# Moving small steps between engines in the front body of a state-space layer

## The reference

```python
xr, gate = jnp.split(x @ W_in.T, 2, axis=-1)
xr = xr + t_emb[:, None, :]
xc = jax.nn.silu(conv(xr, W_conv) + b_conv)          # 4 taps in time, each channel by itself
xn = (xc - xc.mean(-1)) / jnp.sqrt(xc.var(-1) + 1e-05) * ln_g + ln_b
Bm, Cm, dt = jnp.split(xn @ W_xproj.T, 3, axis=-1)
dt = jnp.tanh(dt @ W_dt.T + b_dt) * 0.01
Ad = 1.0 + dt * (-jnp.tanh(A_log))
Bd = Bm * jnp.minimum(jnp.linalg.norm(xn, axis=-1, keepdims=True), 1.0)
# scan over time: h = clip(h * ad + bd * xt, -10, 10);  yt = ct . h
y = ys + D * xn
x = x + (y * jax.nn.silu(gate)) @ W_out.T
```

## Time and profile before

| | |
|---|---|
| median of 3 runs | 1788.49 us (1788.26 to 1793.8) |
| span of the profiled execution | 1790.3 us |
| the profiled execution's own time beside its span | the profile gives none; its span is 1.8 us above the median |
| TensorE busy | 1677.0 us, 94% |
| VectorE busy | 1623.9 us, 91% |
| ScalarE busy | 1307.1 us, 73% |
| GpSimd busy | 686.9 us, 38% |
| first root step of the front stage to first scan step, first layer | 568.03 to 743.08 us |

### The profile page before, as it was taken

The page is one execution under the profiler, slowest core; times in us unless marked ns, Lnnn a source line. Parts: engine busy times, 40 slices in busy tenths (PEclk is TensorE's granted clock), DMA queues, the critical chain, the costliest instruction groups (busy, mean ns, idle before and its releaser), DMA issues. The chain is left out here.

```text
span 1790.3 us, 43798 instructions
## 1 busy us (share of the span) xinstructions
PE 1677.0 (94%) x14852; PEld 748.9 (42%) x14852; DVE 1623.9 (91%) x2492; ACT 1307.1 (73%) x2213; POOL 686.9 (38%) x702
## 2 busy tenths in 40 slices
PE   6999999999999999889999999999998899999998
PEld 3555555555554555332222224545553322222244
DVE  5899999999987999989999998679999899999975
ACT  5655556455546999889999993069998899999910
POOL 0223233232332332456666650012335576765500
PEclk9999999999999999899999999999998999999999
DMA  4000001000002344554545666624345445455678
GB/s 162 1 2 0 1 2 31 2 1 0 1 1 83 129 161 163 181 172 133 183 150 188 226 188 205 237 84 173 136 175 185 155 137 184 150 189 196 189 235 276
DMA packets 126456, 226.85 MB, mean 127 GB/s; under 512 B 35620, under 2 KB 61220, under 8 KB 117540
## 3 DMA queue, kind: packets, MB, share of 16 engines
q1 hardware_dynamic: 125912, 223.51, 37.9%
q10 hardware_dynamic: 432, 1.84, 0.3%
HBM read 141.95 MB, written 83.36 MB: 126 GB/s over the span
## 5 line engine op out<-in xcount | busy, mean ns | idle before, releaser
L1063 ACT ACTIVATE R<-q,Ast 128x512 f32<-128x512 f32 x1016 | 632.9, 708 | 34.5 <-DVE q L2085 32.3
L2085 DVE SCALAR_TENSOR_TENSOR q<-R,PS 128x512 f32<-128x512 f32 x1008 | 610.3, 677 | 9.6 <-ACT R L1063 5.9
L628 POOL TENSOR_TENSOR Uw<-Ub,rowmask 96x512 bf16<-96x512 bf16 x256 | 335.6, 1345 | 144.0 <-PE PS L1510 131.7
L1510 PE MATMUL PS<-xq,Uw 97*128 97x512 bf16 x1024 | 327.1, 391 | 46.5 <-DVE q L2085 37.8
L1527 PE MATMUL PS<-q,Wy 128*32 128x512 f32 x2016 | 279.8, 610 | 0.4 <-DVE q L2085 0.4
L1510 PEld LDWEIGHTS PS<-xq,Uw 97*128 97x128 bf16 x1024 | 84.9, 97 | 363.5 <-DVE q L2085 271.4
L1178 PE MATMUL PS<-X,Win 128*128 (+1 forms) x456 | 213.6, 606 | 0.1
L1079 PE MATMUL PS<-xn,Wl 128*128 128x512 f32 x384 | 186.6, 609 | 0.8 <-DVE xn L1649 0.7
L549 POOL TENSOR_TENSOR ex<-ex,rs 128x1024 f32<-128x1024 f32 x32 | 76.8, 2401 | 164.2 <-DVE rs L1672 164.2
L1767 DVE SCALAR_TENSOR_TENSOR acc<-xp,Wc,acc 128x512 f32<-128x512 f32 x192 | 134.5, 749 | 2.6 <-DVE eC L1889 0.2
L542 POOL TENSOR_TENSOR vsc<-vTd,vs_t 128x1024 f32<-128x1024 f32 x16 | 41.6, 2601 | 216.4 <-ACT vTd L773 216.4
(11 more groups left out here) (183 smaller groups left out, 2640.9 us busy)
## 6 DMA issues: line engine op xcount, KB each, us to landing
xq<-xpart_d SPq DMA_DIRECT2D x384, 192.0 KB
sg_d<-sg SPq DMA_DIRECT2D x16, 1024.0 KB, 5.3
xn_d<-z SPq DMA_DIRECT2D x16, 1024.0 KB, 3.9
y_d<-ys SPq DMA_DIRECT2D x64, 256.0 KB, 4.0
xnp<-xn_d SPq DMA_DIRECT2D x16, 1024.0 KB, 8.3
sgp<-sg_d SPq DMA_DIRECT2D x16, 1024.0 KB, 11.1
xpart_d<-xh SPq DMA_DIRECT2D x16, 512.0 KB, 2.9
xpart_d<-xmi SPq DMA_DIRECT2D x16, 512.0 KB, 3.7
```

The lines of the kernel that those rows point to most:

```text
L628: pl.tensor_tensor(Uw[0:XROWS, h, w, :, :, :], Ub[0:XROWS, w, 0:N, ds(s0, CH)].rearrange("p n t -> p t n").unsqueeze(2).broadcast_to([XROW ...
L1063: act.activation((end if end and (h, t) == (1, CH - 1) else R)[:, w, :], q[:, t % 2, w, :], ACT.Relu, scale=Ast[:, h, w, t:t + 1], bias=CL ...
L1510: pe.matmul(PS[:, w, :], Uw[0:KROWS, h, w, t, :, :].rearrange("p b n -> p (b n)"), xq[0:KROWS, hb, w, s8 % XT, :], start=True, stop=True). ...
L2085: v.scalar_tensor_tensor(out=q[:, s8 % 2, w, :], in0=R[:, w, :], scalar=2 * CLIP, in1=PS[:, w, :], op0=ALU.min, op1=ALU.subtract).then_inc ...
```

## The change

It moves steps of the front body from one engine to another and reorders the lists around them.

- `inverse_norm` and VectorE's `over_decay` leave the bodies; GpSimd gets `norm_over_decay`, five steps that give the same `mr`. `carried` goes to GpSimd too.
- In the six looped bodies `split_b` is divided: ScalarE makes the first part (`b_high`), VectorE the next two steps (`b_rest`), GpSimd the last part (`b_low`). In the seventh body it stays whole on VectorE.
- `mean_middle` goes from GpSimd to ScalarE. In the looped bodies two of the four casts of `middle_part` go from ScalarE to GpSimd.
- On VectorE `decay` stands ahead of the last conv product, `rest(it, 3, 3)` ahead of `mean_rows`, and `scaled_b` between the second and third `centred`.
- On ScalarE `high_part(3)` and `mean` stand ahead of `log_norm`, and `tap(it + 1, 3)` ahead of the second gate.
- On TensorE the first gate projection is the one that is split in halves (its first half at the end of the body before), no longer the third; the mean's spread stands ahead of the third input projection.
- SyncE no longer waits for `xmi_r` before it stores the x parts; `xlo_r` stands for it.

```diff
+                def parts_free(it):
                     pl.wait_ge(xq_st, it * 48 + 48)
-                    pl.wait_ge(eC_r, it + 1)
                     alone(pl)
...
+                def middle_part(it, k, cast):
+                    pl.wait_ge(xr1_r, it * TT + k + 1 + TT)
+                    alone(pl)
+                    pl.tensor_copy(xmi[:, k, :], xr1[:, k, :]).then_inc(xmi_r, 1)
+                    pl.wait_ge(xmi_r, cast)
+                    pl.tensor_tensor(xlo[:, k, :], xr1[:, k, :], xmi[:, k, :], ALU.subtract).then_inc(xlo_r, 1)
+
+                def low_part(it, k, cast):
+                    pl.wait_ge(xma_r, cast)
+                    pl.tensor_tensor(xlo[:, k, :], xr1[:, k, :], xmi[:, k, :], ALU.subtract).then_inc(xlo_r, 1)
+
+                def norm_over_decay(it):
+                    pl.wait_ge(n2_r, it + 1)
+                    pl.wait_ge(ng_r, it * 2 + 2)
+                    alone(pl)
+                    pl.tensor_tensor(n3[:, :], n2[:, :], mn[:, :], ALU.mult).then_inc(mn_r, 1)
+                    pl.wait_ge(mn_r, it * 3 + 1)
+                    pl.tensor_tensor(n4[:, :], n3[:, :], mn[:, :], ALU.mult).then_inc(mn_r, 1)
+                    pl.wait_ge(rc_r, it * 4 + 4)
+                    pl.tensor_tensor(n3[:, :], n3[:, :], rc[:, :], ALU.mult).then_inc(mm_r, 1)
+                    pl.wait_ge(mn_r, it * 3 + 2)
+                    alone(pl)
+                    pl.tensor_scalar(n4[:, :], n4[:, :], -0.5, 1.5, ALU.mult, ALU.add).then_inc(mn_r, 1)
+                    pl.wait_ge(mm_r, it + 1)
+                    pl.wait_ge(mn_r, it * 3 + 3)
+                    alone(pl)
+                    pl.tensor_tensor(mr[:, :], n4[:, :], n3[:, :], ALU.mult).then_inc(mr_r, 1)
...
+                def b_low(it):
+                    pl.wait_ge(tv_s, it * 4 + 3)
+                    pl.tensor_tensor(tvp[:, 2, :], tvr[:, :], tvp[:, 1, :], ALU.subtract).then_inc(tv_s, 1)
...
                     over_decay(l * G + g)
-                    mean_middle(l * G + g + 1)
-                    last_parts(l * G + g)
+                    parts_free(l * G + g)
+                    middle_part(l * G + g, 0, g * 2 + (l * (2 * G) + 1))
+                    norm_over_decay(l * G + g)
+                    middle_part(l * G + g, 1, g * 2 + (l * (2 * G) + 2))
+                    carried(l * G + g)
+                    low_part(l * G + g, 2, g * 2 + (l * (2 * G) + 1))
+                    low_part(l * G + g, 3, g * 2 + (l * (2 * G) + 2))
+                    b_low(l * G + g)
...
+                def b_high(it):
+                    act.wait_ge(tv_st, it * (TV_STORES * 16) + TV_STORES * 16)
+                    act.wait_ge(tok_mm, it + 1)
+                    act.activation(tvp[:, 0, :], PS[:, 7, 0:P], ACT.Copy).then_inc(tv_s, 1)
...
                     gate_silu(it + 1, 0)
+                    tap(it + 1, 3)
                     gate_silu(it + 1, 1)
-                    tap(it + 1, 3)
...
                     logarithm_set()
-                    log_norm(it)
                     high_part(it, 3, 3)
                     mean(it + 1)
+                    log_norm(it)
+                    mean_middle(it + 1)
                     minus_c(it)
...
                     square(it + 1, 3)
+                    if ahead:
+                        b_high(it)
...
-                    gate_in(it + 1, g + 1, 0)
                     variance(it, 0, 4)
...
                     x_in_proj(it, g, 3)
+                    gate_half(it + 1, g + 1, 0, 1)
                     gate_in(it + 1, g + 1, 1)
-                    gate_half(it + 1, g + 1, 2, 0)
                     pe.wait_ge(row_r, it * 2 + (2 * AT + 2))
                     spread_out(5, rows3, zb_mm)
-                    gate_half(it + 1, g + 1, 2, 1)
+                    gate_in(it + 1, g + 1, 2)
...
                     if ahead:
                         x_in_proj(it + 1, g + 1, 1)
+                    pe.wait_ge(row_r, it * 2 + (2 * AT + 3))
+                    spread_out(5, rows3, zm_mm)
                     if ahead:
                         x_in_proj(it + 1, g + 1, 2)
-                    pe.wait_ge(row_r, it * 2 + (2 * AT + 3))
-                    spread_out(5, rows3, zm_mm)
+                        gate_half(it + 2, g + 2, 0, 0)
                     fold_b(it)
...
+                    decay(it)
                     conv(it + 1, 2, 3)
-                    decay(it)
...
                     rest(it, 2, 2)
-                    inverse_norm(it)
                     mean_rest(it + 1)
-                    over_decay(it)
-                    scaled_b(it)
-                    carried(it)
+                    rest(it, 3, 3)
                     mean_rows(it + 1)
-                    rest(it, 3, 3)
                     centred(it + 1, 0)
                     centred(it + 1, 1)
+                    scaled_b(it)
                     centred(it + 1, 2)
                     centred(it + 1, 3)
                     if ahead:
                         embed(it + 2, g + 2, 1)
-                    if ahead:
                         embed(it + 2, g + 2, 2)
-                    split_b(it)
+                        b_rest(it)
+                    else:
+                        split_b(it)
```

More of the change, by code:

```diff
@@ L236, in cond_resid_kernel @@
              "xlo_ready", "xparts_stored")]
+        xma_r = sem("xmid_by_scalar")
         dlg_r, dco_g, rg_r, zg_r, ng_r, mm_r = [sem(n) for n in
@@ L577, in _ @@
                 pl.memset(words(pass_tables[0][0]), 0.0).then_inc(tab0_zero, 1)
-                def last_parts(it):
+                def parts_free(it):
                     pl.wait_ge(xq_st, it * 48 + 48)
-                    pl.wait_ge(eC_r, it + 1)
                     alone(pl)
-                    for k in range(TT):
-                        pl.wait_ge(xmi_r, it * TT + k + 1)
-                        pl.tensor_tensor(xlo[:, k, :], xr1[:, k, :], xmi[:, k, :], ALU.subtract).then_inc(xlo_r, 1)
+                def middle_part(it, k, cast):
[4 more added lines that the diff above has]
+                    pl.tensor_tensor(xlo[:, k, :], xr1[:, k, :], xmi[:, k, :], ALU.subtract).then_inc(xlo_r, 1)
@@ new lines, in carried @@
+                def carried(it):
+                    pl.wait_ge(rB_r, it + 1)
+                    pl.tensor_tensor(eC[:, :].rearrange("p (b t) -> p b t", t=S)[:, :, 0:S - 1],
+                                     Cn[:, :].rearrange("p (b t) -> p b t", t=S)[:, :, 0:S - 1],
+                                     rB[:, :].rearrange("p (b t) -> p b t", t=S)[:, :, 1:S], ALU.mult).then_inc(eC_r, 1)
+                def b_low(it):
+                    pl.wait_ge(tv_s, it * 4 + 3)
+                    pl.tensor_tensor(tvp[:, 2, :], tvr[:, :], tvp[:, 1, :], ALU.subtract).then_inc(tv_s, 1)
@@ L605, in std_middle @@
                     pl.wait_ge(rem_r, it * 2 + (2 * AT + 2))
-                    alone(pl)
-                    pl.tensor_copy(middle[:, :], remain[:, :]).then_inc(mid_r, 1)
-                def mean_middle(it):
-                    pl.wait_ge(rem_r, it * 2 + (2 * AT + 1))
                     alone(pl)
@@ L652, in _ @@
                 over_decay(l * G + G - 2)
-                mean_middle(l * G + G - 2 + 1)
+                norm_over_decay(l * G + G - 2)
+                carried(l * G + G - 2)
                 pl.wait_ge(tab_in[0], l * (16 * TABLES) + 16 * TABLES)
@@ L659, in _ @@
                     stage(0, 0, h, True)
-                last_parts(l * G + G - 2)
+                parts_free(l * G + G - 2)
+                for k in range(TT):
+                    low_part(l * G + G - 2, k, l * (2 * G) + 2 * (G - 2) + k + 1)
                 with pl.Fori(1, 4) as c2:
@@ L674, in _ @@
                     for k in (2 * c2, 2 * c2 + 1):
-                        pl.wait_ge(xmi_r, it * TT + k + 1)
+                        pl.wait_ge(xmi_r, l * (2 * G) + 2 * (G - 2) + k + 1)
                         pl.tensor_tensor(xlo[:, k, :], xr1[:, k, :], xmi[:, k, :], ALU.subtract).then_inc(xlo_r, 1)
@@ L987, in body @@
                         tap(it + 2, 0)
-                    middle_part(it, 0)
-                    middle_part(it, 1)
+                    else:
+                        middle_part(it, 0)
+                        middle_part(it, 1)
                     middle_part(it, 2)
@@ L1457, in _ @@
                 into(l * G + 1, 1, 2, xr_mm)
+                gate_half(l * G + 1, 1, 0, 0)
                 with pe.Fori(0, G - 2) as g:
@@ L1965, in rest, with b_rest @@
                     v.tensor_tensor(xr1[:, k, :], PS[:, bank, :], xh[:, k, :], ALU.subtract).then_inc(xr1_r, 1)
+                def b_rest(it):
+                    v.wait_ge(tv_s, it * 4 + 1)
+                    v.tensor_tensor(tvr[:, :], PS[:, 7, 0:P], tvp[:, 0, :], ALU.subtract).then_inc(tv_s, 1)
+                    v.wait_ge(tv_s, it * 4 + 2)
+                    v.tensor_copy(tvp[:, 1, :], tvr[:, :]).then_inc(tv_s, 1)
                 def split_b(it):
```

7 lines of the change are left out of this document (1 added, 6 removed).

## The result

| | before | changed |
|---|---|---|
| median of 20 runs each | 1792.96 us (1788.25 to 1797.94) | 1787.63 us (1783.12 to 1796.11) |
| span of the profiled execution | 1790.3 us | 1785.4 us |
| VectorE busy, first 1366 us (both front stages) | 1236.4 us | 1224.5 us |
| GpSimd busy, the same | 476.5 us | 528.4 us |

The ratio is 0.9975, with a 95% interval of 0.9965 to 0.9986: 4.5 us saved by the ratio, 5.3 by the medians, where 6.4 was forecast. The time of 1787.63 is 5.5 us over the predicted 1782.1. But 4.5 of these are the kernel before, whose median is 1792.96 over twenty runs and was 1788.49 over the three that the forecast started from; only 1.1 is gain that did not come. The time is in the range, but the gain stays within 0.3%, where the likeliest case had it just beyond.

What follows compares the result with a forecast made beforehand. VectorE was taken to bound the front-stage bodies, with a loop over several engines next. Savings of 4.6 (bodies), 1.8 (first bodies) and 0 (last bodies) make 6.4 us: from 1788.49 to 1782.1 us, range 1773 to 1792.

Steps and rivals of the forecast that it cites:

- the likeliest case: Looped bodies: the GpSimd chain sets a body of 24.4 to 24.9 us, time 1779 to 1785; chance 0.45.
- What bounds: Front-stage body: VectorE bounds at 23.6 of 25.0 us; once relieved, a loop through several engines takes over.
- Where the loop closes: Front-stage body: moved work forms a chain round to the next root(1), guess `mn` in time at 17.4; body 24.65 us.
- VectorE's 2.35 us: VectorE in a body: eight instructions leave, together 2.35 us; on VectorE alone the body would fall to 22.7.
- The chain up to the fold: Over_decay to `carried` on GpSimd: `mr` ready at 19.95, `carried` starts at 21.75 behind middle_part 1, done at 22.2.
- From the fold to root(1): TensorE and ScalarE at the body's end: b_high starts at 22.7, then tap, Ln and Exp; root step at 24.4.
- The meetings at the end: VectorE beside GpSimd's low parts: 0.15 us for b_rest's cast and 0.1 for root(2); body 24.65.
- My sign for dearer meetings: Changed profile: b_rest's cast or `mean_rows` taking over 0.6 us would show meetings dearer than taken.
- The split gate at 0 in later bodies: TensorE in later bodies: as much gate work from variance to the deviation's spread as before, so 0.
- First and last bodies: Each layer's ends: first body gains 0.88 us, 1.8 over two layers; last body 0, bounds 0.5 less and 1 more.
- The slower one: Looped bodies: each meeting lasts a whole subtraction, body up to 26.6; slower beyond 0.3% from 25.6 on; chance 0.12.
- the rival of no change: Looped bodies: chain 0.3 to 0.6 longer, body 25.0 to 25.2, only first bodies gain; 1787 to 1789; chance 0.28.

Runs made afterwards that it cites:

- The two kernels that make Ln start 0.1 earlier: Changed kernel with b_high behind the next body's tap on ScalarE, or b_high back on VectorE: 1788.37 us (ratio 0.9978) and 1786.37 us (single run).

## Why the prediction was right and wrong

**What bounds.** Right as far as the engines go. VectorE's relief put a loop over GpSimd, TensorE and ScalarE in its place. TensorE waits for `carried` in each body, and with that link cut the body falls to 23.88.

**Where the loop closes.** This step failed. I closed the loop from the fold through b_high, the tap, Ln and Exp to root(1), counted everything from root(1), and took the guess `mn` as in time, so that GpSimd would not wait for it. In the changed kernel TensorE's order sets the pace: 19.25 us without a gap from the fold to the end of the mean's sums. The guess hangs behind these sums, ready at 17.69 instead of 17.4, and GpSimd waits 0.27 for it in each body. root(1) has 0.3 to 0.4 us to spare. The two kernels that make Ln start 0.1 earlier show it: their bodies are 24.78 and 24.79 all the same. My own loop can be put together from the runs: 22.09 from root(1) to the fold where GpSimd does not wait for `mn` (the kernel without TensorE's part) and 2.44 from the fold to root(1), 24.53 together at most. It is there, and it is shorter than the one that counts. So it is in part luck that 24.65 lies only 0.14 from 24.79. That the guess is the link is read from the rows; no run moved it alone. The change itself put `high_part(3)` and `mean` ahead of the guess on ScalarE, and an order with the guess first, which could win back up to the 0.27, was not tried.

**VectorE's 2.35 us.** The eight instructions are gone, 2.3 us of busy time, but VectorE's busy time in a body fell only from 23.62 to 22.34. Most of the difference of 1.0 is the cast of the second B part, 0.8 us longer in its meeting; the mean's rows (0.42 instead of 0.34) and twelve conv products (755 instead of 750 ns) add 0.14. None of it counted, since VectorE no longer set the end.

**The chain up to the fold.** Right in its links on GpSimd, and 0.19 late: over_decay's first step met the conv product as forecast; the guess `mn` kept GpSimd waiting 0.27 where I had it in time, so that norm_over_decay began at 17.87 instead of 17.5; middle_part 1 stood ahead of `carried` for 1.75.

**From the fold to root(1).** This term was mis-sized too, but as seen it did not set the body. I had Ln at 23.6, behind the tap on ScalarE, and the variance sums done 1.34 after the fold's start. ScalarE's tap came 0.42 behind b_high instead of 0.16 and took 0.72. (Between the two lies the end of the loop's body; in the middle of it a tap follows a small copy after 0.16, at 660.71 behind 660.55. The cause was not tested.) In the two kernels without b_high in the way Ln starts 1.61 after the fold, when TensorE's sums are done. From the forecast start of 22.2 that alone is 23.8; from the measured 22.39 it is 24.0, and Ln came at 24.11.

**The meetings at the end.** The 0.25 us (cast 0.15, root(2) 0.1) did not count. The cast met a low part and took 1.04, but root(1) was later still; root(2) took 0.29. My sign for dearer meetings, a cast over 0.6, came true without a cost. In the body shown (24.83 against 24.65) Ln is 0.51 later and root(1) follows it 0.33 sooner than I had it. A meeting costs the whole rest of the other's instruction, as the Trainium skill has it (SBUF, State Buffer, section SBUF: two separate sides); the traces agree with 1.20 us for a root step of 0.29.

**The split gate at 0 in later bodies.** Wrong as a price of the edit. I counted the matmuls from the variance sums on, and left out the whole projection between the fold and these sums, which the edit takes away. The sum itself had the sums right behind the fold already, so 0 was right as a term beside it. The edit alone costs 0.4 a body; inside the change it is worth 1.64 a body.

**First and last bodies.** The first gained 0.86 and 0.96, as forecast 0.88 each. The last gained 0.04 and 0.18, within the bounds around 0. So the term that came short is that of the bodies, 3.3 instead of 4.6: 0.22 a body in the first layer and 0.33 in the second, instead of 0.38.

**The rivals.** The slower one did not come with this order. The two kernels with the root on VectorE show its mechanism at full size: 1.0 to 1.2 us for a step of 0.29, and 2% of the kernel. The ratio of the Trainium skill (GPSIMD Engine Reference, section Elementwise, side-by-side cycle accounting), 1.96 times VectorE, is given there for an add over 2048 elements, not for a product over 128 as the prediction put it; for these the changed kernel shows 0.45 to 0.46 us against 0.29, 1.6 times. A body of 25.2 did not come. By the time alone, 1787.63 would fit the rival of no change (1787 to 1789) too; the body of 24.79 lies in the forecast's 24.4 to 24.9 and not in that rival's 25.0 to 25.2. The time fits both only because the kernel before gave 1788.49 in its first three runs and 1792.96 in twenty.

## What to carry to other kernels

When the bound engine is relieved, walk the new loop to its end on every engine, and see at each fork which of the parallel lines ends last. An engine that works without a gap is such a line too, and times counted from another engine's step hide it. Here the loop gave back all but 0.2 to 0.3 of what VectorE had lost. A link in that loop must not stand behind work that nobody waits for: a carried product of 0.4 us behind 1.75 us of other work cost more than it had freed, and back on the engine that had just been relieved it brought the body from 24.79 to 24.08. And price an edit inside the change, not alone: half a projection was a loss of 0.4, a gain of 1.64 or nothing, according to who waited beside it.

## What was not expected of the hardware

Where VectorE and GpSimd met, the later one ended 0.14 to 0.16 us after the other's instruction, and in both directions: GpSimd's 128x128 scalar step took 0.56 instead of 0.30 beside a conv product (656.08 and 0.75 long), VectorE's root steps 1.01 to 1.20 instead of 0.29 beside subtractions of 1.15 to 1.16. A VectorE cast from one SBUF tile to another was held as well (1.04 instead of 0.23, to 0.09 after the low parts' end).

With the root on VectorE two neighbouring bodies differ by 0.7 us with the same work, and TensorE's granted clock (the third number from the end, of 1.00 for 2.4 GHz) with them:

```profile
652.33:680.16 27.83, 24.81 (x256) 13.69 (x255) 24.82 (x46) 22.68 (x43) 8.48 (x13) 1.00 0.38 140
680.16:708.66 28.50, 25.66 (x256) 14.13 (x255) 24.93 (x46) 22.90 (x43) 8.49 (x14) 0.94 0.41 143
```

0.94 is a mean over the body, so part of it ran at the lower level of 1.2 GHz. TensorE waits 2.8 us for the rows in every body of this kernel, but what follows the wait is not the same. TensorE's timeline behind the wait in each of the two:

```profile
673.69 0.40 PE L1394 MATMUL PS<-rows,spread 128*128 128x128 bf16 x4 [2.83 <-DVE rows L1949]
673.93 1.94 PE L1221 MATMUL PS<-X,Win 128*128 x4
...
701.53 0.40 PE L1394 MATMUL PS<-rows,spread 128*128 128x128 bf16 x4 [2.84 <-DVE rows L1949]
701.76 2.87 PE L1221 MATMUL PS<-X,Win 128*128 x4
```

Of the twelve such waits in the two loops, six are followed by four matmuls that take 2.6 to 3.5 us together, and six by four that take 1.94; the granted clock of the body is 0.94 for the former and 1.00 for the latter. In the changed kernel, where TensorE waits 0.6 in a body, all six bodies of the first loop show 1.00, and so does the kernel before. So a wait of TensorE can cost a second time here, and does not each time. What decides it was not found.
